# Fp16 rows, transposing DMA loads and three bank sets in a four-part transformer kernel with a routed expert layer

## What is computed

```python
x = x + tanh(g_xattn[0]) * LN(x) * scan(0.9, ctx * ctx)        # decayed running sum
x = x + tanh(g_ffn[0])   * adapters(LN(x))   # W product, and the winning one of 4 low-rank adapters
x = x + tanh(g_xattn[1]) * attention(LN(x), ctx)               # 16 heads, sigmoid, masked
x = x + tanh(g_ffn[1])   * moe(LN(x))
def moe(x2):                               # 4096 tokens, 8 experts, the best 2 for each
    top_p, top_e = top_k(softmax(x2 @ router_w), 2)
    y_e = gelu(x2 @ w_in[e] + b_in[e]) @ w_out[e] + b_out[e]
    return sum over the 2 chosen of top_p * y_e
```

## Time and profile before

| | |
|---|---|
| median of 3 runs | 474.13 us (472.04 to 478.74) |
| the profiled execution | 474.49 us, its span 472.6 us |
| busy in the span | PE 394.9, DVE 368.8, ACT 331.4, POOL 268.7 us |
| TensorE clock granted, mean | 0.969 |
| DMA | 87.10 MB, mean 184 GB/s |

### The profile page before, as it was taken

How to read it: one execution, slowest core, us unless ns; L and a number is a source line. 1 busy time by engine, 2 the same in 40 slices (tenths; PEclk the granted TensorE clock), 3 DMA queues, 4 the chain that set the end, 5 groups by cost and what they waited for, 6 DMA issues and landing times.

```text
span 472.6 us, 13099 instructions
## 1 busy us (share of the span) xinstructions
PE 394.9 (84%) x4092; PEld 308.3 (65%) x4092; DVE 368.8 (78%) x1416; ACT 331.4 (70%) x671; POOL 268.7 (57%) x313
## 2 busy tenths in 40 slices
PE   2758899998999989999899987789559999979850
PEld 1536667776776777677686765568438897967740
DVE  2888888998988889899789786367655667779994
ACT  2855788898889889898879877566706666646640
POOL 2522112545454364626545565769988888888870
PEclk9998999999999999999999999899959999999996
DMA  7245576664565555875553774624335569396985
GB/s 242 83 139 163 180 214 179 196 181 141 177 213 170 166 171 167 221 204 184 180 174 111 223 220 121 198 68 130 101 126 143 170 175 332 116 341 251 323 275 204
DMA packets 69500, 87.10 MB, mean 184 GB/s; under 512 B 9485, under 2 KB 55290, under 8 KB 69306
## 3 DMA queue, kind: packets, MB, share of 16 engines
q1 hardware_dynamic: 60074, 65.81, 46.7%
q0 software_dynamic: 6816, 18.65, 10.8%
q10 hardware_dynamic: 2544, 1.81, 1.2%
HBM read 51.07 MB, written 35.18 MB: 182 GB/s over the span
## 4 chain that ended last, share of the span: by engine, by line
PE 42%; POOL 17%; issue 14%; DVE 10%; DMA 8%; ACT 6%; ACTq 0%; POOLq 0%; DVEq 0%; SPq 0%
PE ps_J L1650 12%; PE ps_F L1650 6%; POOL store_y L771 6%; DMA store_y<-y_out,y_row 6%; PE ps_O L1764 5%; PE ps_T L1659 5%; POOL store_x L765 5%; PE ps_S L1751 5%; POOL pause_t L778 5%; PE ps_R L1689 2%; PE ps_O L1775 2%; PE ps_G L1650 2%; DMA temp_t<-in_temp 1%; DVE y_out L2934 1%; DVE xb_lo L2903 1%
## 5 line engine op out<-in xcount | busy, mean ns | idle before, releaser
L771 POOL DMA_INDIRECT store_y<-y_out,y_row x78 | 81.4, 1044 | 21.8 <-issue 16.5
L765 POOL DMA_INDIRECT store_x<-xn_E,slot_u x64 | 68.0, 1063 | 26.5 <-DVE slot_u L2633 13.6
L1089 ACT ACTIVATE prob<-ps_S 128x512 f32<-128x512 f32 x128 | 72.4, 594 | 12.7 <-PE ps_S L1751 10.0
L778 POOL TENSOR_TENSOR pause_t<-half_ones,minus_half 128x2 f32<-128x2 f32 x71 | 54.7, 770 | 1.9
L1751 PE MATMUL ps_S<-q_stack,k_stack 128*128 128x256 f16 x256 | 44.5, 276 | 5.9 <-issue 3.8
L2922 DVE TENSOR_TENSOR h_lo<-h_f,h_hi 128x512 f16<-128x512 f32 x39 | 26.9, 689 | 21.0 <-ACT h_hi L1173 9.4
L1650 PE MATMUL ps_J<-wout_hi,h_hi 128*128 x112 | 31.2, 278 | 14.3 <-DVE y_out L2934 10.9
L1764 PE MATMUL ps_O<-prob,v_wide 128*32 128x128 f32 x1024 | 41.0, 279 | 1.1 <-ACT prob L1089 0.5
L1165 ACT ACTIVATE h_f<-ps_F,bin_t 128x256 f32<-128x256 f32 x56 | 23.4, 470 | 24.5 <-PE ps_F L1650 18.9
L751 POOL TENSOR_TENSOR rstd_C<-var_C,minus_half 128x2 f32<-128x2 f32 x16 | 12.1, 759 | 40.4 <-DVE var_C L2412 40.4
L1650 PE MATMUL ps_F<-xb_hi,win_hi 128*128 128x256 f16 x112 | 31.7, 283 | 3.9 <-DVE xb_lo L2903 3.3
(11 more groups left out here) (301 smaller groups left out, 1399.5 us busy)
## 6 DMA issues: line engine op xcount, KB each, us to landing
parts_scratch<-parts SPq DMA_DIRECT2D x32, 256.0 KB
k_stack<-parts_scratch SPq DMA_DIRECT2D x64, 128.0 KB
q_stack<-parts_scratch SPq DMA_DIRECT2D x128, 64.0 KB
xb<-store_x SPq DMA_DIRECT2D x30, 257.0 KB
y_got<-store_y SPq DMA_DIRECT2D x14, 512.0 KB
c_in<-in_ctx SPq DMA_DIRECT2D x16, 256.0 KB
x_in<-in_x SPq DMA_DIRECT2D x16, 256.0 KB
store_x<-zeros SPq DMA_DIRECT2D x15, 257.0 KB, 4.6
```

What stands on the lines that cost most here:

```text
L765: pool.indirect_dma_start(store_x, bass.IndirectOffsetOnAxis(slot_u[q][:, at:at + 1], 0), xn_e[q][:, at, :], None).then_inc(s_scat[q], 16)
L771: pool.indirect_dma_start(store_y, bass.IndirectOffsetOnAxis(y_row[n][:, b:b + 1], 0), y_out[n][:, b, :], None).then_inc(s_y_kept[n], 16)
L778: pool.tensor_tensor(pause_t[:, :], half_ones[:, :], minus_half[:, 0:2], ALU.pow).then_inc(s_set_p, 1)
L1089: act.activation(prob[m % PROBS][:, 2 * n:2 * n + 2, :, :], bank_s[n], ACT.Sigmoid, scale=float(HD) ** -0.5).then_inc(s_prob[n], 1)
```

## The change

It does the following.

- **Rows**: the layer norm E is made twice. DVE writes it as fp32 into a scratch (`normed_e`, two tensor_scalar a pair), ACT writes its fp16 rounding straight into the rows (`rows_hi`, twice each), and POOL subtracts the one from the other into the second half of each row (`rows_lo`, 128x1024 elements a pair). A row in `store_x` has the same 257 words, but holds 256 fp16 hi, 256 fp16 lo and the row number.
- **Router**: `transpose_e`, `hi_e` and `lo("E")` are gone. SP issues two transposing DMAs a pair from the rows in SBUF into `xt_e` (`turn_rows`), and `logits` waits for them.
- **Blocks**: `load_block` is a transposing DMA of 256 rows x 512 fp16 and a small DMA for the row numbers. `transpose_block`, `copy_hi` and `copy_lo` are gone; `layer1` reads the loaded tile. A buffer is free when `layer1` has read it, not when it is transposed.
- **Banks**: three sets for all blocks (F and J, S0 and S1, R and O), and three buffers instead of two for the hidden parts.
- **Order**: all streams are reordered, the block stage too, which is written out. Of the pauses, 6 are left from the first block's scatter on. The scatters of pair 15 come after those of block 6, not of block 2. At the start the loads of `x` and `decay` come before those of `ctx` and `ident`, and TensorE starts with `scan(0)`. On DVE `hidden_lo(38)` comes before `take_rows(38)` and its wait.

```diff
+            def turn_rows(p):
+                need(sp, s_logits, p)
+                sp.wait_ge(s_rows_lo, p + 1)
+                for b in range(2):
+                    sp.dma_start(xt_e[:, b, :, :], xn_e[p % 2][:, TOP * b, 0:D].bitcast(F16), transpose=True)                        .then_inc(s_t["E"], 16)
...
                 for j in [j for j in range(i) if home(j) == n][-1:]:
-                    sp.wait_ge(s_xb_t, j + 1)
+                    sp.wait_ge(s_h, j + 1)
                     sp.wait_ge(s_y_row, j + 1)
-                sp.dma_start(xb[n][:, :, :], store_x[bass.ds(row_at(i, 0), BLK), :]
-                             .rearrange("(p b) c -> p b c", b=SUB))\
-                    .then_inc(s_xb[n] if n < XB else s_late[(n - XB) // GROUP], 16)
+                at, done = row_at(i, 0), s_xb[n] if n < XB else s_late[(n - XB) // GROUP]
+                sp.dma_start(xb[n][:, :, :], store_x16[bass.ds(at, BLK), 0:2 * D], transpose=True).then_inc(done, 16)
+                sp.dma_start(row_no[n][:, :, :], store_x[bass.ds(at, BLK), D - 1:WIDE].rearrange("(b p) c -> p b c", b=SUB))\
+                    .then_inc(done, 16)
...
         def side(i):
-            return 0 if i <= EARLY else (i - EARLY) % 2
+            return i % HB
...
+            def rows_lo(p):
+                pool.wait_ge(s_rows_hi, 2 * p + 2)
+                pool.wait_ge(s_xn["E"], 2 * p + 2)
+                pool.tensor_tensor(e_lo[p % 2], xn_f[p % 2].unsqueeze(2).broadcast_to([128, 2, TOP, D]), e_hi[p % 2],
+                                   ALU.subtract).then_inc(s_rows_lo, 1)
...
+            def normed_e(p):
+                q = p % 2
...
+                dve.wait_ge(s_rstd["E"], p + 1)
+                need(dve, s_rows_lo, p - 1)
+                for b in range(2):
+                    dve.tensor_scalar(xn_f[q][:, b, :], xs[:, 2 * p + b, :], mv["E"][q][:, b, 0:1], rstd["E"][q][:, b:b + 1],
+                                      ALU.subtract, ALU.mult).then_inc(s_xn["E"], 1)
...
-                    pe.wait_ge(s_xb_lo, i + 1)
+                    loaded(pe, i)
                     need(pe, s_gelu, KT * used_up_to(i))
...
-            for i in range(4, TILES):
-                keep_block(i, 0)
-                if i < CLOSE:
-                    long_pause()
-                keep_block(i, 1)
+            keep_block(4, 0)
+            keep_block(4, 1)
+            long_pause()
+            keep_block(5, 0)
+            keep_block(5, 1)
+            keep_block(6, 0)
+            keep_block(6, 1)
+            scatter(15, 3)
+            scatter(15, 0)
+            scatter(15, 1)
+            scatter(15, 2)
+            keep_block(7, 0)
+            keep_block(7, 1)
```

More of the change, by code:

```diff
@@ L413, in build, with last_at @@
         block = st.enter_context(nc.Block())
+        store_x16 = store_x.bitcast(F16)
         def side(i):
-            return 0 if i <= EARLY else (i - EARLY) % 2
+            return i % HB
+        def last_at(k):
+            return max(i for i in range(TILES) if side(i) == k)
         def home(i):
@@ L970, in _ @@
             keep_block(1, 1)
+            scatter(14, 0)
             long_pause()
@@ new lines, in _ @@
+            layer1(7, 0)
+            layer1(7, 1)
+            ranks(("logits", 15), 15)
+            layer2(5, 0)
+            layer2(5, 1)
+            layer1(8, 0)
+            layer1(8, 1)
+            layer2(6, 0)
+            layer2(6, 1)
+            layer1(9, 0)
+            layer1(9, 1)
+            layer2(7, 0)
+            layer2(7, 1)
+            layer1(10, 0)
+            layer1(10, 1)
+            layer2(8, 0)
+            layer2(8, 1)
+            layer1(11, 0)
+            layer1(11, 1)
@@ L3915, in _ @@
             router_both(15)
-            hidden_lo(4)
+            take_rows(5)
             add_bias(3)
-            copy_lo(6)
+            add_bias(4)
+            router_diff(15)
             rank_rows(15)
             rank_picked(15)
-            take_rows(6)
+            hidden_lo(6)
+            hidden_lo(7)
+            next(final)
+            next(final)
+            next(final)
+            take_rows(6)
+            add_bias(5)
+            add_bias(6)
+            take_rows(7)
+            next(final)
+            next(final)
+            next(final)
+            next(final)
             next(final)
@@ L3946, in _ @@
             next(final)
-            hidden_lo(7)
-            next(final)
-            add_bias(6)
-            copy_lo(9)
-            next(final)
-            next(final)
-            take_rows(9)
             next(final)
@@ L3981, in _ @@
-            for n in range(TILES + 1 - ADD_AT, NP):
-                add_pair(n)
+            next(final)
+            next(final)
+            take_rows(11)
+            next(final)
+            hidden_lo(11)
+            next(final)
+            add_bias(10)
+            hidden_lo(12)
+            hidden_lo(13)
+            take_rows(12)
+            take_rows(13)
+            add_bias(11)
+            take_rows(14)
+            add_bias(12)
+            take_rows(15)
+            hidden_lo(14)
@@ new lines, in _ @@
+            hidden_lo(15)
+            add_bias(13)
+            hidden_lo(16)
+            add_bias(14)
+            take_rows(16)
+            take_rows(17)
+            hidden_lo(17)
+            take_rows(18)
+            add_bias(15)
+            hidden_lo(18)
+            take_rows(19)
+            add_bias(16)
+            hidden_lo(19)
+            next(gates)
+            hidden_lo(20)
+            add_bias(17)
+            hidden_lo(21)
+            take_rows(20)
+            next(gates)
@@ new lines, in _ @@
+            add_bias(18)
+            add_bias(19)
+            hidden_lo(22)
+            add_bias(20)
+            next(gates)
+            take_rows(21)
+            take_rows(22)
+            hidden_lo(23)
+            next(gates)
+            add_bias(21)
+            add_bias(22)
+            next(gates)
+            take_rows(23)
+            hidden_lo(24)
+            hidden_lo(25)
+            take_rows(24)
+            add_bias(23)
+            add_bias(24)
+            next(gates)
+            hidden_lo(26)
@@ new lines, in _ @@
+            hidden_lo(27)
+            take_rows(25)
+            add_bias(25)
+            next(gates)
+            take_rows(26)
+            add_bias(26)
+            take_rows(27)
+            hidden_lo(28)
+            take_rows(28)
+            hidden_lo(29)
+            add_bias(27)
+            hidden_lo(30)
+            add_bias(28)
+            next(gates)
+            take_rows(29)
+            take_rows(30)
+            take_rows(31)
+            hidden_lo(31)
+            add_pair(0)
@@ new lines, in _ @@
+            add_bias(29)
+            add_bias(30)
+            add_bias(31)
+            add_pair(1)
+            add_pair(2)
+            hidden_lo(32)
+            hidden_lo(33)
+            add_pair(3)
+            add_pair(4)
+            take_rows(32)
+            add_bias(32)
+            add_pair(5)
+            take_rows(33)
+            add_bias(33)
+            hidden_lo(34)
+            add_pair(6)
+            add_pair(7)
+            take_rows(34)
+            hidden_lo(35)
+            add_bias(34)
```

2319 lines of the change are left out of this document (1282 added, 1037 removed).

## The result

| | median of 4 runs | lowest, highest | profiled execution |
|---|---|---|---|
| before | 473.09 us | 471.82, 478.74 | span 472.6 |
| changed | 485.26 us | 482.57, 485.92 | 485.92, span 484.0 |

The ratio is 1.0223 (95% interval 1.013 to 1.0316): slower than before, where 446.5 us was predicted. Whether it is slower by more than 2% the interval leaves open.

The account below looks back on a forecast made before the run. No single engine bounds the pair stage (TensorE fullest); POOL bounds the block stage. 310.6 + 113.5 + 8 + 12.8 = 444.9 us span, adjusted to 446.5 us; own range 439 to 456, overall 428 to 484.

Parts of the forecast that it names:

- The step that failed: Pair stage: POOL's new subtraction of 1024 elements, 2.3 us a pair, stays hidden if inverse roots don't stand behind it.
- The 8 us of gain: Pair stage: TensorE's lost transposes and ACT's lost copy give 0.5 us a pair, 8 us over 16, between 0 and 11.
- Rival B: Pair stage gives nothing: POOL's subtraction and added links make inverse roots, then DVE, 0.5 us a pair late; 458 us, chance 0.18.
- Router's slack: Pair stage: the router's later transposing DMAs do no harm, since its rows are used for ranks a full pair later.
- The block stage: POOL bounds it before; changed, 113.5 us of POOL work between first and last scatter, plus 8 of waits (3 to 20).
- The transfers: Block stage: a transposing load takes 1.1 us against 0.88 plain; DMA engines busy 129 of 137 us, tight but not the bound.
- rival A: Block stage: transfers become the bound; 490 us at 2.28 us a transposing load, about 550 at 3.76; chance 0.20.
- rival A's far end: Block stage: a block's eight tiles run one after the other through DMA; above 700 us, 0.03 of A's 0.20.
- The sum: Whole kernel: 310.6 to the first block scatter, 113.5 of POOL work, 8 of waits, 12.8 of tail: 444.9 us span.
- the tail: After the last scatter's start: landing, a load, the sums of four pairs and a store, left at 12.8 us.

Follow-up runs that it names:

- `lo_tiny`: The changed kernel with POOL copying only 2 of 256 columns of the rows' low halves from pair 2 on: 469.13 us, ratio 0.9895.
- `lo_one_input`: The changed kernel with POOL's subtraction of the rows replaced by a one-input copy of the same 1024 elements: 470.84 us, ratio 0.9997.
- `lo_tiny_turn_early`: `lo_tiny` with SP issuing the router's transposing DMAs of pairs 3 and 12 ahead of the stacked queries of pairs 5 and 14: 468.04 us, ratio 0.989.
- `before_sub`: The kernel before with an added, unused POOL subtraction of 128x1024 a pair, ahead of the adapter's inverse norm: 499.55 us, ratio 1.0553.
- `before_no_pause`: The kernel before without the 43 POOL pauses from the first block's scatter on: 461.76 us, ratio 0.9742.
- `take_late`: The changed kernel with each DVE `take_rows` from block 8 on moved right ahead of the same block's `add_bias`: 492.15 us, ratio 1.0368.
- `plain_loads`: The changed kernel with the transposing block loads replaced by plain loads of the same rows, left untransposed: 480.85 us, ratio 1.0213.
- `outputs_early`: The changed kernel with the first five output loads issued between block loads 32 to 37 instead of behind them on SP: 489.17 us, ratio 1.0325.

## Why the prediction was wrong

**The step that failed** is "POOL gains a subtraction ... hidden while the order keeps inverse roots from standing behind it". Its length was right (2.3 taken, 2.07 measured), and POOL had the room (9 to 10 of 17 us busy). I asked who waits for POOL, and not whom POOL's instruction stops without a wait. Against -8 us the pair span came out at +24.9:

- 14.9 us are the hold (`lo_tiny`; 14.0 by `lo_one_input`). It is 0.93 a pair, while the single holds are 1.1 to 2.1 long and lengthen DVE's busy time by 19.1: a part of it was slack.
- 5.3 us more are SP's order (`lo_tiny_turn_early`): 7.3 us of gap at one place, with TensorE's hole and the lower clock behind it, less 2.3 that the exchange of pair 12 takes back. It is near the spread of single executions, and the ratio doesn't show it.
- 4.7 us still stand between 252.9 and before's 248.2. Three gaps are longer than before's: from input 1 to 2 (17.1 for 14.7), 13 to 14 (17.3 for 13.4) and 14 to 15 (19.1 for 16.7). The second is made by the exchange of pair 12 itself, as shown above; the changed kernel has 13.1 there. The other two stay open. TensorE's waits for `xt_lo_C` are one candidate: 7.3 us in the changed kernel, still 7.4 in `lo_tiny_turn_early`, and 1.8 before, so neither the hold nor SP's order makes them. Then it would be the new order, which no run isolates.
- The 8 us of gain never came, even so. TensorE did lose some of it as work (223.0 us busy in the pair span of `lo_tiny_turn_early`, 227.2 before, where 16 x 0.48 = 7.7 was the term), but four engines stand close together there, and DVE lost nothing: its two normalising passes take 411 ns each and overlap, 0.74 a pair for the 0.7 taken and the 0.69 saved.

The Trainium skill says it ("GPSIMD Engine Reference", section 1, Specifications): GpSimd shares its SBUF interfaces with VectorE, with contention for VectorE instructions that have two SBUF inputs or run in a 2-port mode. The trace agrees for the first kind, and shows how long the contention lasts: the VectorE instruction stands until GpSimd's is over, 2.02 us for 0.16. `var_A` in `before_sub` was held with a single SBUF input; whether it ran in such a mode no run here shows.

**Rival B** had the right stage and named POOL's subtraction and the added links, with a loss of 0.5 to 1 us a pair against the forecast. It was (24.9 + 8) / 16 = 2.1. Its mechanism (inverse roots late) is not what the changed kernel shows: DVE's instructions are held, and don't wait. It is what `before_sub` shows, where I had put the instruction ahead of `inv_norm`.

**Router's slack.** "The router has slack: its rows are used for ranks a full pair later" looked at the wrong reader. `logits` has a fixed place in TensorE's stream, and everything behind it waits.

**The block stage** was read rightly and its waits were too small. That POOL was the bound is shown by `before_no_pause`. (With the true last scatter at 461.11, POOL's waits there come to 142.5 - 133.6 = 8.9 us and not to 7.7, which changes nothing.) The pace is as worked out: `layer1` of two successive blocks starts at 412.40 and 415.02, 2.62 us apart, and TensorE is busy 40.00 of 40 us from 392 on. Of the block span of 129.8 the 113.5 are work by the prediction's own terms, so the waits are 16.3 where I took 8, between 3 and 20. In the trace POOL waits 15.1 us for `y_out`, the sums of `add_bias`, between its first and last scatter of blocks, and 5.2 before. Two of the waits lie here, in the chain from 353 to 391:

```profile
357.39 3.83 DMA store_y<-y_out,y_row
...
361.32 0.16 DVE y_row L3218
...
363.54 0.69 DVE h_lo L3227
364.36 2.74 PE ps_O L1857 x12
...
382.85 3.95 DMA store_y<-y_out,y_row
...
386.88 0.06 DVE y_row L3218
386.99 0.70 DVE h_lo L3227
387.82 2.74 PE ps_O L1857 x12
```

Twice a scatter's landing of 3.8 to 4 us holds `take_rows`, `hidden_lo` behind it, and TensorE. Then the layers run at the lower clock for a while (granted 0.50 from 364 to 367 and from 387.8 to 390.5; 2.74 us for 1.31). The prediction kept this wait for block 38 alone. `take_late` shows that another place in DVE's order doesn't free it, since block loads hang on the same step. The transposing loads don't make it longer: `take_rows` waits 13.1 us for landings in the changed kernel and 13.3 in `plain_loads`.

**The transfers** cost more than I took and aren't the bound, as against rival A: a transposing load has by the estimate above 0.74 us over a plain one, where 0.22 was taken (bounds 0 to 2.9). The DMA share is 0.80 to 1.00 in the block stage, 0.85 to 0.95 forecast, and `plain_loads` gives 4.2 us. That the eight tiles of a block run one after the other is refuted: SP issues a block every 2.20 us on average from 402 to 429 and TensorE waits for none of them.

Against rival A's far end the Trainium skill ("VectorE: DVE Perf Modes", The three transpose paths) has 1309 ns for one tile of 128x128; here eight of them and a small load are issued every 2.20 us and TensorE, which takes a block in 2.62, waits for none, so that figure is no rate of a long transfer.

**The sum** of 444.9 became 484.0: 32.9 us from the pair stage (-8 became +24.9), 8.3 from the block span (121.5 became 129.8), 0.2 from the tail (12.8 became 13.0), less 2.3 at the start and between the last attention input and the first scatter of a block.

## What to carry to other kernels

Before work goes to an idle engine, ask also what it stops while it runs. GpSimd at half load is no free place for long elementwise instructions beside a full VectorE: compare VectorE's mean durations of tiny two-operand instructions before and after, since a hold looks like work there and not like a wait. In an order written by hand, each new producer with a long latency has to be placed in the stream of the queue that issues it, and be judged by the fixed place of its first reader. Whatever it is put ahead of then waits for it as well: one of the two exchanges here gave, and the other took. And where an engine paced by filler is the bound, try first without the filler: in the block stage that alone gave as much as the whole change (129.0 and 129.8 us of block span).

## What the runs showed of the hardware

- While a GpSimd elementwise instruction of 128x1024 runs (2.07 us, 1.03 as a copy), a VectorE instruction with two SBUF operands that starts behind it doesn't end before it. Those that read PSUM, reductions and reciprocals pass. `var_A`, with one SBUF input and a constant, was held (`before_sub`). It goes the other way as well: in `lo_one_input` a VectorE addition of 128x512 began 0.05 us ahead of GpSimd's copy (247.51) and took its usual 0.68 us, and the copy took 1.53 us for 1.04. Beside GpSimd's short instructions in the kernel before the same ones have 164 (`lg`) and 187 ns (`picks`).
- The subtraction of 128x1024 elements takes GpSimd twice as long as the copy of one input.
- A transposing DMA occupies SP for about 1.2 us (1.23 to 1.32 from 400 to 430 in the changed kernel), a plain one mostly for 0.35 to 0.45. Single ones take longer: a plain one 1.34 (430.12), a transposing one 3.67 (`outputs_early`, 438.08, beside the output loads). A transposing DMA of the router landed 4.78 us after the start of its issue (134.11).
- A hole of 3 to 6 us in TensorE is followed by a layer at 2.3 to 2.7 us for 1.31, at a granted clock of 0.50 (changed kernel, 140 to 142, 364 to 367 and 387.8 to 390.5).
